# Output products of the 32 small experts: tokens as the moving operand, in two column halves

## The reference

```
idx = argmax(xf @ router_w.T + router_b)        # one of 32
h   = relu(xf @ W1[idx] + b1[idx])              # 16 hidden values
out = relu(h @ W2[idx] + b2[idx])               # 64 values, added to the residual
```

## Time and profile before

| | us |
|---|---|
| median of three runs | 5130.27 |
| profiled execution | 5131.49 |
| its span | 5129.4 |
| TensorE busy | 4133.1 (81%) |
| VectorE busy | 2799.5 (55%) |
| ScalarE busy | 2249.6 (44%) |
| granted TensorE clock, mean | 0.87 |
| L1670, all four batches | 87.0 |
| L1671, all four batches | 30.9 |
| L1664, all four batches | 43.8 |

### The profile page before, as it was taken

One profiled execution on the slowest core, in us unless ns is written; L12 is line 12 of the kernel. 1 busy time (PEld: TensorE's weight loads), 2 busy tenths in 40 slices (PEclk: granted clock), 3 DMA queues, 4 the chain that ended last, 5 costly groups with the idle time before them and its releaser, 6 DMA issues. The chain is left out here.

```text
span 5129.4 us, 70930 instructions
## 1 busy us (share of the span) xinstructions
PE 4133.1 (81%) x26920; PEld 2787.2 (54%) x26920; DVE 2799.5 (55%) x6139; ACT 2249.6 (44%) x3791; POOL 493.5 (10%) x824
## 2 busy tenths in 40 slices
PE   6786866899887875899888875899887875899888
PEld 4664644465546544565546544565546554565546
DVE  4554737355545738355545748355545747355544
ACT  3342647154332548244342558244332548244332
POOL 0000010201100010201100010111100010111100
PEclk9898877799888987799898987799998987799988
DMA  2000000000000000000000000000000000000000
GB/s 88 3 3 17 1 17 1 0 1 1 1 1 4 1 17 1 0 1 1 1 1 4 1 17 1 0 1 1 1 1 4 1 1 1 0 1 1 1 1 4
DMA packets 28313, 26.52 MB, mean 5 GB/s; under 512 B 10550, under 2 KB 26934, under 8 KB 27450
## 3 DMA queue, kind: packets, MB, share of 16 engines
q1 hardware_dynamic: 27962, 21.98, 1.5%
HBM read 20.40 MB, written 1.57 MB: 4 GB/s over the span
## 5 line engine op out<-in xcount | busy, mean ns | idle before, releaser
L719 ACT ACTIVATE big<-ps,negmax 128x1024 f32<-128x1024 f32 (+1 forms) x672 | 600.1, 899 | 267.6 <-DVE negmax L752 267.6
L752 DVE TENSOR_REDUCE negmax<-ps 128x1 f32<-128x1536 f32 x336 | 589.8, 1757 | 39.2 <-PE ps L622 19.6
L705 ACT COPY big<-ps 128x512 f32<-128x512 f32 x672 | 394.1, 586 | 494.0 <-PE ps L646 490.9
L646 PE MATMUL ps<-cst,big 128*128 128x128 f32 x4032 | 502.8, 275 | 30.3 <-ACT big L719 29.8
L646 PEld LDWEIGHTS ps<-cst,big 128*128 128x128 f32 x4032 | 457.3, 142 | 48.0 <-ACT big L719 39.7
L436 ACT COPY xt<-ps 64x512 f32<-64x512 f32 x144 | 78.9, 579 | 817.7 <-PE ps L428 817.7
L423 PE MATMUL ps<-cst 128*128 128x512 f32 x608 | 324.3, 692 | 128.2 <-DVEq L190 58.2
L615 PE MATMUL ps<-kup,qup 128*128 128x512 f32 (+3 forms) x768 | 360.3, 566 | 41.8 <-POOLq L190 41.0
L408 POOL TENSOR_TENSOR st<-st,cst 128x6 f32<-128x6 f32 x104 | 156.7, 1507 | 2188.6 <-DVE st L396 2184.5
L662 PE MATMUL ps<-big,v 128*32 128x128 f32 (+1 forms) x8064 | 321.9, 277 | 8.1 <-DVE ctxt L1243 6.0
L615 PE MATMUL ps<-klo,qlo 128*128 128x512 f32 (+3 forms) x672 | 313.7, 550 | 3.8 <-DVE big L705 1.6
(11 more groups left out here) (391 smaller groups left out, 7400.5 us busy)
## 6 DMA issues: line engine op xcount, KB each, us to landing
rw<-in_w_route SPq DMA_DIRECT2D x128, 64.5 KB, 1.9
cst<-in_consts SPq DMA_DIRECT2D x1, 2671.0 KB, 14.7
cst<-in_consts SPq DMA_DIRECT2D x1, 2670.5 KB, 8.8
big<-in_consts SPq DMA_DIRECT2D x1, 1872.5 KB, 21.9
out_dram<-res SPq DMA_DIRECT2D x4, 384.0 KB, 2.8
experts_in<-in_consts SPq DMA_DIRECT2D x1, 1360.0 KB, 17.5
qup<-in_patches SPq DMA_DIRECT2D x4, 260.0 KB
klo<-in_pe_low SPq DMA_DIRECT2D x2, 384.0 KB, 23.2
```

Source lines behind the costliest of these rows:

```text
L646: ins = nc.tensor.transpose(turned_bank(kind, u, g)[:, i * P:(i + 1) * P], prob[:, slot_of(kind, u), (4 * g + i) * P:(4 * g + i + 1) * P], ...
L705: copy(pt[:, slot_of(kind, u), g, 0:n], turned_bank(kind, u, g)[:, 0:n]).then_inc(*ph.mark(copier(kind, g)))
L719: nc.scalar.activation(prob[:, slot_of(kind, u), cols], src[:, cols], ACT.Exp, bias=bias, accum_out=part_sum[:, u, k:k + 1]).then_inc(*ph. ...
L752: nc.vector.tensor_reduce(negmax[:, u:u + 1], flat[:, 0:n], AX.X, ALU.max, negate=True)\
```

## The change

The output products are turned round. For each block of 512 tokens the weights are stationary (64 columns of `w2_2` per chunk) and the 512 tokens of `hid` move. Chunks 0 and 2 accumulate in PSUM partitions 0 to 63, chunks 1 and 3 in partitions 64 to 127 of the same bank (4 or 5); the bias product goes to the lower half. ScalarE copies the bank to `both_halves` (free space in `qup`); twelve products, one per tile, with the copied tile as weights and `fold[64]` moving add the halves and bring the tokens back to the partitions, into banks 6 and 7. The order on TensorE is hidden(0), hidden(1), outputs(0), hidden(2), outputs(1), added(0), outputs(2), added(1), added(2). ScalarE's copies stand after the second and the fourth activation of the last block, and at the end.

```
+                def add_halves(j):
+                    act.wait_ge(*ph.after("halves_psum", j + 1))
+                    nc.scalar.copy(both_halves[:, 512 * j:512 * (j + 1)], ps[:, 4 + j % 2, :]).then_inc(*ph.mark("halves_copied"))
                 for i in range(NB * C2):
                     ...
+                    if j == NB - 1 and c in (1, 3):
+                        add_halves(c // 2)
+                add_halves(2)
...
-                pe.wait_ge(*ph.after("hid_ready", NB * C2))
-                for t in range(T):
-                    o = ps[:, 4 + t // 6, (t % 6) * D:(t % 6 + 1) * D]
+                def hidden(j):
+                    pe.wait_ge(*ph.after("xt_copied", NB + j + 1))
                     for c in range(C2):
-                        nc.tensor.matmul(o, hid[:, c, t * P:(t + 1) * P], K("w2_2")[:, c * D:(c + 1) * D], start=(c == 0), stop=False)
-                    ins = nc.tensor.matmul(o, xt2[64:96, t * P:(t + 1) * P], K("b2_2")[64:96, :], start=False, stop=True)
-                    if t % 6 == 5:
-                        ins.then_inc(*ph.mark("out_psum"))
+                        if j > 0:
+                            pe.wait_ge(*ph.after("hid_ready", (j - 1) * C2 + c + 1))
+                        nc.tensor.matmul(ps[:, c, :], K("w1_2")[:, c * P:(c + 1) * P], xt2[:, 512 * j:512 * (j + 1)],
+                                         start=True, stop=True).then_inc(*ph.mark("hid_psum"))
+                def outputs(j):
+                    pe.wait_ge(*ph.after("hid_ready", (j + 1) * C2))
+                    if j > 1:
+                        pe.wait_ge(*ph.after("halves_copied", j - 1))
+                    for c in range(C2):
+                        strip = ps[D * (c % 2):D * (c % 2) + D, 4 + j % 2, :]
+                        nc.tensor.matmul(strip, K("w2_2")[:, c * D:(c + 1) * D], hid[:, c, 512 * j:512 * (j + 1)],
+                                         start=(c < 2), stop=(c == C2 - 1), skip_group_check=True)
+                    nc.tensor.matmul(ps[0:D, 4 + j % 2, :], K("b2_2")[64:96, :], xt2[64:96, 512 * j:512 * (j + 1)],
+                                     start=False, stop=True, skip_group_check=True).then_inc(*ph.mark("halves_psum"))
+                def added(j):
+                    pe.wait_ge(*ph.after("halves_copied", j + 1))
+                    for t in range(4 * j, 4 * j + 4):
+                        ins = nc.tensor.matmul(ps[:, 6 + t // 6, (t % 6) * D:(t % 6 + 1) * D], both_halves[:, t * P:(t + 1) * P],
+                                               fold[D][:, :], start=True, stop=True)
+                        if t % 6 == 5:
+                            ins.then_inc(*ph.mark("out_psum"))
...
-                    nc.vector.scalar_tensor_tensor(h[:, 6 * i:6 * i + 6, :], rows_bank([4, 5], i), 0.0, h[:, 6 * i:6 * i + 6, :],
+                    nc.vector.scalar_tensor_tensor(h[:, 6 * i:6 * i + 6, :], rows_bank([6, 7], i), 0.0, h[:, 6 * i:6 * i + 6, :],
```

More of the change, by code:

```diff
@@ L75 @@
     "moe2": {"rstd_ready": 2, "xt_copied": 6, "hid_ready": 12, "xt_psum": 6, "logit_psum": 1, "hid_psum": 12,
-        "out_psum": 2, "vec_step": 18, "var_ready": 2, "normed": 2},
+        "out_psum": 2, "halves_psum": 3, "halves_copied": 3, "vec_step": 18, "var_ready": 2, "normed": 2},
     "rel3a": {"pool_step": 8, "upper_cleared": 1, "rstd_ready": 4, "rot_used": 6, "xt_copied": 3, "qv_ready": 6,
@@ L286, in build @@
         sparse = work
+        both_halves = qup[:, 1, :]
         qt = qlo[:, 0, :]
@@ L1657, in _ @@
                 transpose_pe(ph, xa, [4, 5, 6], width=P)
[L1658 to L1665, removed]
@@ new lines, in added @@
+                def added(j):
[5 more added lines that the diff above has]
+                            ins.then_inc(*ph.mark("out_psum"))
+                hidden(0)
@@ L1674, in _ @@
+                hidden(1)
+                outputs(0)
+                hidden(2)
+                outputs(1)
+                added(0)
+                outputs(2)
+                added(1)
+                added(2)
                 ph.leave(pe)
```

## The result

The changed kernel takes 5060.1 us (median of four runs, 5055.6 to 5071.1) against 5132.2 for the kernel before (5117.7 to 5139.9): ratio 0.9868, 95% interval 0.9846 to 0.9889. Two later comparisons, each on one chip, gave 0.9889 (0.9871 to 0.9906) and 0.9873 (0.9852 to 0.9893). The prediction of 5062.5 us lies 2.4 us off. The profiled execution took 5059.0 us, its span is 5056.8.

A forecast was written before the change was run, and what follows sets the result against it. TensorE alone was taken to bound the stage. Hidden 10.7, output 8.6 and adding products 3.1 make 22.4 us, with tail and handover 22.6 instead of 39.5; saving 67.7 over four batches gives 5062.5 us, range 5046 to 5084.

The forecast's parts named there:

- The removed products: Old output tiles of the second expert layer: two at 1.39 us, one of 2.36, nine at 2.51, 27.7 us a batch.
- The hidden products: Twelve before and after, unchanged in shape; splitting them into three calls costs nothing, 10.7 us a batch.
- Halves side by side: New output products: a pair in both PSUM halves costs one product's 0.86 us, a block 2.86, three blocks 8.6.
- rival A: Output products: halves don't run side by side, a block takes 4.6 us instead of 2.86, 21 more in all; chance 0.07.
- rival C: Weight loads of the new output products stay in the open: 2.5 us a batch, 10 in all, 5072.5; chance 0.03.
- The adding products: Twelve products adding the halves, three groups of 1.03 us at full clock, 3.1 us a batch.
- The copies: ScalarE's three copies, 0.59 us each, all hidden, the third behind added(1); if nothing hid them, 2.1 us a batch.
- The clock: Full clock assumed for the whole changed stretch; later clock steps worth up to 8 us in all either way.
- rivals B: Clock falls at the stage's end, before the adding products: some 16 us in all, 5078; chance 0.06.
- Rival D: Low clock stays for the whole stretch, 43.7 us against 39.5, 17 slower in all, 5147; chance 0.02.
- Behind the stage: Next stage: dummies take 12.9 us instead of 15.7, TensorE stands some 8.4 for VectorE; nothing won.
- The sum: Changed stretch 22.6 us instead of 39.5, saving 16.9 a batch, 67.7 over four, median 5062.5 us.

The follow-up runs named there:

- dummies12: Kernel before with a 512-column dummy product after each of the twelve output tiles; stretch 38.0 us against 39.5, whole 5124.9 us in one run.
- one_half: Changed kernel with all four chunks accumulating in PSUM partitions 0 to 63; ratio 0.9935 to the kernel before, stretch 27.9 us.
- narrow: Changed kernel with each 512-column output product cut into four of 128 moving columns; ratio 0.9907 to the kernel before, stretch 22.9 us.
- adds_early: Changed kernel with added(1) laid before outputs(2); stretch 23.5 us against 22.8, whole 5041.2 us in one run.
- again2: Changed kernel unaltered, run once more on one chip with a later paired-bias version; ratio 0.9873 to the kernel before, median 5059.6 us.
- pair_order: Changed kernel with the chunks of a block in the order 0, 2, 1, 3; stretch 22.8 us, whole 5054.6 us in one run.
- dummies4: Kernel before with a 512-column dummy product after every third output tile, four a batch; ratio 1.0049, stretch 44.6 us against 39.5.

## Why the prediction was right

- **The removed products.** Nine tiles at the low clock. Right, and dummies12 shows that the clock and not the number of products made them dear: 11.0 of 16.7 us.
- **The hidden products.** Forecast 10.7, measured 11.1: 7.48 for the first eight and 3.63 (925.87 - 922.24) for hidden(2), whose four products alone are 3.44. I had said that splitting them costs nothing; the 0.19 us over are the passage from the bias's form into theirs and on to that of the strips, which I had counted on the side of the output products alone. The first eight are over by another 0.2. This is the one term that was put too low.
- **Halves side by side.** A block at 2.86 us, measured 2.87; one_half gives 4.58 for rival A's 4.6. The row that carried it was L847, the same form with fewer columns.
- **Weight loads (rival C).** L1683's loads take 0.137 us in the median, and narrow quadruples them for 0.03 us a block. By the Trainium skill, "TensorE: Matmul & The Clock Gate", Part 3, they should not overlap where the row group is the same; the measured 2.90 us decides against it here. The same part of the Trainium skill also lets a load for the background weight buffer run ahead of the products, which would fit; no run here tells by which way the loads were hidden.
- **The adding products.** Forecast 1.03 a group, measured 929.77 - 928.74 = 1.03. The last two groups and the handover to VectorE take 2.04 (934.67 - 932.63), 0.2 less than forecast, which makes up for half of what the hidden products were short.
- **The copies.** The third hides behind added(1); with that cover taken away (adds_early) TensorE stands 0.68 us and the stretch grows by 0.7, as priced.
- **The clock.** Held through the stage in every trace of the change (rivals B and D); that the new products would hold it was carried over from one stretch of similar ones, and nothing here says what it takes. (The row of 512-column products that I described ends at added(0), not at added(1); outputs(2) follows it.) The start is not always at the same point: in the first batch 3.3 us were low, not 1.0, and the stretch came to 23.9 us at a clock of 0.93, outside the 23.5 and the 0.97 that I had allowed; again2 shows the same in its first batch (23.8).
- **Rival D's price.** A slip: 21.98 us of work doubled and 0.2 of tail are 44.2 us, not 43.7, so some 19 us slower instead of 17. Nothing hung on it.
- **Behind the stage.** Nothing was won there, as forecast. The dummies take 13.1 us (forecast 12.9), TensorE stands 8.15 (8.4). I gave 21.4 us from the last addition to L428; it is 21.9 in both kernels, a slip in reading.
- **The sum.** A stretch of 22.6 us forecast, 22.8 measured; 67.7 us in all forecast, 65.8 in the first pair of traces, 66.4 by the mean of two and three traces. That the median came within 2.4 us is partly luck: the rest of the span moves by more than that from run to run, and the three comparisons, by their ratios, put the gain at some 68, 57 and 65 us.

## What to carry to other kernels

When a row of small products lies in a stretch at half clock, price it at both clocks before pricing its shape: here two thirds of the gain was that the new products kept TensorE at 2.4 GHz, and the stretch with the old form got 1.5 us shorter when eleven useless products were added to it. If the result is narrow (64 columns), make the weights the narrow side, let 512 tokens move, and share the products out to the two halves of PSUM, since that is the other third; a small product with an identity stack brings the tokens back for 0.26 us a tile. Lay a finished group of such products in front of the wait for the last copy.

## What the runs showed of the hardware

The time outside the changed stage comes in steps. From the last addition of the changed stage to the end of the attention "attn3b", with the same instructions, the nine traces of the change and its variants have 377.0 to 377.1 us, 379.8 to 380.1, or 381.0 to 382.4. The shortest step goes with less time at the low clock, 23.9 us by the trace's record of it. The other two both have 30.7 to 34.1 us, so that time doesn't tell them apart; what does was not found. Windows over that section in the second batch, first again2 (34.1 us low), then adds_early (23.9):

```profile
2081.80:2463.20 381.40, 352.57 (x2536) 214.48 (x2536) 214.05 (x419) 170.78 (x327) 63.11 (x127) 0.96 0.00 1
```

```profile
2079.30:2456.30 377.00, 349.89 (x2536) 211.90 (x2536) 214.03 (x418) 170.78 (x327) 63.13 (x127) 0.97 0.00 1
```

ScalarE and VectorE do the same work to 0.03 us; only TensorE differs, by 2.7 us of busy time in the 4.4. In the short version the clock fell for 3.4 us right behind the changed stage, and some 18 us behind it was low for 6.8 us where the others have 13.6 to 20.5. The short version was there once in one_half (first batch). In adds_early the short version came in all four batches, some 18 us in all, which is most of why it is the fastest single run though its stage is 0.7 us longer. Whether that would come again was not tried; its one run can't show it. The stretch with the sparse attention behaves likewise: from the last product of "sim2" to the first hidden product, the third batch has 201.6 to 207.0 us over the fourteen traces. Over all fourteen traces the rest of the span lies between 4945 and 4984 us, so an edit worth under some 20 us in this kernel is to be read from the stretch it touches, not from the total.

Products for the two halves need not stand next to each other in the text to run together (pair_order, a block of 2.87 us in either order).

A TensorE that is busy all the time can still be at the low clock: the old output products were at 1.2 GHz in 932.1 to 956.8, with TensorE busy in all of it. With a 512-column dummy after each tile the clock stayed at 2.4 GHz (dummies12); with one after each third tile it fell (dummies4).
